# Sixteen batches of a stage written out instead of a two-batch loop, with every wait on a constant

## The reference, cut to what matters

```python
x = x + causal_attention(layernorm(x))     # stage 0: Q, K, V with bias, mask k <= q, softmax, Wo, bo
x = x + split_attention(layernorm(x))      # stage 1: a class per position, attention inside the class
x = x + rotary_attention(layernorm(x))     # stage 2: rotary q and k, softmax over all keys
x = x + split_attention(layernorm(x))      # stage 3: as stage 1
```

## Time and profile before

| | |
|---|---|
| median of 3 runs | 5199.68 us (5198.17 to 5214.73) |
| the profiled execution | 5192.83 us, of which its span is 5191.0 us |
| TensorE clock granted, mean | 0.953 |
| PE busy | 4514.9 us, 87% |
| DVE busy | 3178.9 us, 61% |
| ACT busy | 2550.6 us, 49% |
| POOL busy | 1655.2 us, 32% |
| DMA | 525.68 MB, of which 3.82 MB on queue 8 and 1.14 MB on queue 14 are of the kind "instruction" |

### The profile page before, as it was taken

One profiled execution on the slowest core, in us unless ns is written; L12 is line 12 of the kernel. 1 busy time (PEld: TensorE's weight loads), 2 busy tenths in 40 slices (PEclk: granted clock), 3 DMA queues, 4 the chain that ended last, 5 costly groups with the idle time before them and its releaser, 6 DMA issues. The chain is left out here.

```text
span 5191.0 us, 90278 instructions
## 1 busy us (share of the span) xinstructions
PE 4514.9 (87%) x26116; PEld 1909.3 (37%) x26116; DVE 3178.9 (61%) x6578; ACT 2550.6 (49%) x3362; POOL 1655.2 (32%) x922
## 2 busy tenths in 40 slices
PE   4988988899869999899995999999989599889889
PEld 2444444445413333333332333333333233333333
DVE  3545545455447667676663766666666277777776
ACT  1444444444435554455551655555555265555555
POOL 2354544545422434434434133332333300000000
PEclk8999999999979999999997999999999799999999
DMA  4343434344223334233232223323323322222221
GB/s 148 97 149 125 143 119 145 123 135 135 94 67 104 95 92 120 81 110 107 94 109 81 83 87 116 114 87 104 114 89 103 83 75 84 80 79 80 75 75 51
DMA packets 302300, 525.68 MB, mean 101 GB/s; under 512 B 58340, under 2 KB 236136, under 8 KB 285544
## 3 DMA queue, kind: packets, MB, share of 16 engines
q1 hardware_dynamic: 259432, 485.06, 31.5%
q10 hardware_dynamic: 42496, 35.66, 2.1%
HBM read 316.97 MB, written 201.46 MB: 100 GB/s over the span
## 5 line engine op out<-in xcount | busy, mean ns | idle before, releaser
L923 DVE TENSOR_REDUCE neg_max<-scores 128x1 f32<-128x512 f32 (+3 forms) x4096 | 2490.0, 636 | 1448.8 <-PE scores L1282 856.2
L1141 ACT ACTIVATE probs<-scores_t 128x1024 f32<-128x1024 f32 (+2 forms) x2048 | 1926.3, 947 | 1683.0 <-PE scores_t L1315 1193.9
L1282 PE MATMUL scores<-k_stack,q_stack 98*128 98x512 bf16 (+4 forms) x4096 | 1454.2, 378 | 311.0 <-DVE neg_max L923 216.5
L1315 PE MATMUL scores_t<-q_stack,k_stack 100*128 100x512 bf16 (+3 forms) x4096 | 1211.5, 370 | 130.6 <-DMA q_stack<-shift_rows 72.7
L1336 PE MATMUL o_ps<-probs,values 128*32 128x512 f32 (+1 forms) x8192 | 1039.7, 580 | 0.9 <-issue 0.6
L1282 PEld LDWEIGHTS scores<-k_stack,q_stack 96*128 96x128 bf16 (+1 forms) x4096 | 400.3, 98 | 1721.8 <-DVE neg_max L923 1243.9
L1315 PEld LDWEIGHTS scores_t<-q_stack,k_stack 100*128 100x128 bf16 x4096 | 382.3, 100 | 467.5 <-issue 292.1
L766 POOL TENSOR_TENSOR parts<-qk_f,parts 128x1024 bf16<-128x1024 f32 x128 | 272.3, 2128 | 707.8 <-ACT parts L1184 527.4
L779 POOL TENSOR_TENSOR x_res<-x_res,o_bias_s 128x1024 f32<-128x1024 f32 x32 | 75.6, 2364 | 1054.7 <-DMA x_res<-x_after 1054.7
L786 POOL TENSOR_TENSOR sim_inv<-sim_parts,minus_half 128x64 f32<-128x64 f32 x32 | 337.6, 10550 | 196.1 <-DVE sim_parts L1006 196.1
L737 POOL TENSOR_SCALAR var_eps<-mean_var 128x4 f32<-128x4 f32 x64 | 14.6, 229 | 1082.6 <-DVE mean_var L887 1082.6
(11 more groups left out here) (118 smaller groups left out, 4015.8 us busy)
## 6 DMA issues: line engine op xcount, KB each, us to landing
q_stack<-q_parts SPq DMA_DIRECT2D x1536, 64.0 KB, 2.5
values<-v_stage SPq DMA_DIRECT2D x64, 1024.0 KB, 4.2
values<-values SPq DMA_DIRECT2D x64, 1024.0 KB, 5.4
k_parts<-parts SPq DMA_DIRECT2D x192, 256.0 KB, 2.5
q_parts<-parts SPq DMA_DIRECT2D x192, 256.0 KB, 4.1
k_stack<-k_parts SPq DMA_DIRECT2D x256, 192.0 KB, 3.0
k_stack<-k_parts SPq DMA_DIRECT2D x256, 128.0 KB, 3.1
x_after<-x_res ACTq DMA_DIRECT2D x48, 512.0 KB, 2.9
```

The source lines that it names most:

```text
L923: nc.vector.tensor_reduce(neg_max[:, h % G, t:t + 1], bank[:, 0:n], AX.X, ALU.max, negate=True).then_inc(max_done.sem, 1)
L1141: nc.scalar.activation(probs[c][:, h % G, 0:n], st[i][:, 0:n], ACT.Exp).then_inc(exp_done.sem, 1)
L1282: last = nc.tensor.matmul(bank[:, 0:n], q[0:r, h, t * P:(t + 1) * P], k[0:r, h, 0:n], start=True, stop=kind != CAUSAL)
L1315: last = nc.tensor.matmul(st[i][:, off:off + L - q0], k[0:ROWS, h, kt * P:(kt + 1) * P], q[0:ROWS, h, q0:L], start=True, stop=kind != CAUSAL)
```

## The change

The loop of `run_stage` goes. All 16 batches of each stage are written out one after the other in the program of each engine. `Batch` loses its loop register, every wait is on a constant, every address is a constant, and the increments of "passed" are gone with their semaphore. The work, its order on each engine, the buffers and the tables are as they were. The two functions `loops` and `tail` go. The core of the diff:

```diff
     def __add__(self, k):
-        return Batch(self.s, self.n + k, self.turn)
-
-    def index(self):
-        return self.n if self.turn is None else self.turn * 2 + self.n
+        return Batch(self.s, self.n + k)
 
     def one(self):
-        return bass.ds(self.index(), 1)
+        return slice(self.n, self.n + 1)
...
-def wait_reg(eng, sem, value, still=None):
-    eng.wait_ge(sem, value)
-    if still is not None and not isinstance(value, int):
-        eng.sem_inc(still, 1)
...
     def after(self, B, *label):
-        lab = lambda n: (B.s, n) + label
-        if B.turn is None:
-            return self.at[lab(B.n)]
-        second = self.at[lab(B.n + 2)]
-        d = self.at[lab(B.n + 4)] - second
-        c = second - d
-        assert c > 0 and all(self.at.get(lab(B.n + 2 * i), c + d * i) == c + d * i for i in range(loops(B.s)))
-        return B.turn * d + c
-
-    def wait(self, eng, B, *label, still=None):
-        if B.turn is None and B.n < 0:
-            return
-        wait_reg(eng, self.sem, self.after(B, *label), still)
+        return self.at[(B.s, B.n) + label]
+
+    def wait(self, eng, B, *label):
+        if B.n >= 0:
+            eng.wait_ge(self.sem, self.after(B, *label))
...
             first(Batch(s, 0))
-            body(Batch(s, 0))
-            with eng.Fori(0, loops(s), 1) as i:
-                body(Batch(s, 1, i))
-                body(Batch(s, 2, i))
-            for n in tail(s):
+            for n in range(NB):
                 body(Batch(s, n))
             finish(Batch(s, NB - 1))
```

More of the change, by code:

```diff
@@ L188, with __init__ @@
 class Batch:
-    def __init__(self, s, n, turn=None):
-        self.s, self.n, self.turn = s, n, turn
+    def __init__(self, s, n):
+        self.s, self.n = s, n
     def __add__(self, k):
-        return Batch(self.s, self.n + k, self.turn)
-    def index(self):
-        return self.n if self.turn is None else self.turn * 2 + self.n
+        return Batch(self.s, self.n + k)
     def one(self):
-        return bass.ds(self.index(), 1)
+        return slice(self.n, self.n + 1)
     @property
     def begun(self):
[L206 to L214, removed]
-def wait_reg(eng, sem, value, still=None):
-    eng.wait_ge(sem, value)
-    if still is not None and not isinstance(value, int):
-        eng.sem_inc(still, 1)
+        return self.n > 0
 class Count:
@@ L233, in after, with wait_earlier, skip @@
     def after(self, B, *label):
-        lab = lambda n: (B.s, n) + label
-        if B.turn is None:
-            return self.at[lab(B.n)]
-        second = self.at[lab(B.n + 2)]
-        d = self.at[lab(B.n + 4)] - second
-        c = second - d
-        assert c > 0 and all(self.at.get(lab(B.n + 2 * i), c + d * i) == c + d * i for i in range(loops(B.s)))
-        return B.turn * d + c
-    def wait(self, eng, B, *label, still=None):
-        if B.turn is None and B.n < 0:
-            return
-        wait_reg(eng, self.sem, self.after(B, *label), still)
-    def wait_earlier(self, eng, B, back, *label, still=None):
-        v = self.after(B, *label) - self.step * back
[L253 to L260, removed]
+        return self.at[(B.s, B.n) + label]
+    def wait(self, eng, B, *label):
+        if B.n >= 0:
+            eng.wait_ge(self.sem, self.after(B, *label))
+    def wait_earlier(self, eng, B, back, *label):
+        v = self.after(B, *label) - self.step * back
+        if v > 0:
+            eng.wait_ge(self.sem, v)
+    def skip(self, eng, B, *label):
+        self.wait_earlier(eng, B, 1, *label)
         eng.sem_inc(self.sem, self.step)
@@ L536, in front_before @@
             if f == OWN:
-                if B.turn is None and B.n <= X_AHEAD:
+                if B.n <= X_AHEAD:
                     return (B + (-1), "xt") if B.n else (None, "")
                 return B + (-1 - X_AHEAD), "nx"
-            if B.s == 0 and (B.turn is not None or B.n + X_AHEAD < NB):
+            if B.s == 0 and B.n + X_AHEAD < NB:
                 return B + X_AHEAD, "xt"
@@ L573, in load_x @@
                 if B.begun:
-                    xn_done.wait(sp, B + (-1), OWN, still=still)
+                    xn_done.wait(sp, B + (-1), OWN)
                 sp.dma_start(x_new[:, :, :],
@@ L609, in load_next @@
                 if B.begun:
-                    st_full.wait(sp, B + (-1), H - 1, 1, still=still)
-                    qx_done.wait(sp, B + (-1), still=still)
+                    st_full.wait(sp, B + (-1), H - 1, 1)
+                    qx_done.wait(sp, B + (-1))
                 if B.s == 0:
-                    parts_out["k"].wait(sp, B + 1, OWN, still=still)
-                    parts_out["q"].wait(sp, B + 1, OWN, still=still)
+                    parts_out["k"].wait(sp, B + 1, OWN)
+                    parts_out["q"].wait(sp, B + 1, OWN)
                 load_stacks(B + 1)
@@ L618, in load_next @@
                 if B.begun:
-                    pv_done.wait(sp, B + (-1), NG - 1, T - 1, still=still)
+                    pv_done.wait(sp, B + (-1), NG - 1, T - 1)
                 if B.s == 0:
-                    v_out.wait(sp, B + 1, OWN, still=still)
+                    v_out.wait(sp, B + 1, OWN)
                 load_values(B + 1)
@@ L637, in store_parts @@
                 a, last = (0 if side == "q" else 2), prep_steps(kind_of(B, f))[-1]
-                prep.wait(sp, B, f, side, last, still=still)
+                prep.wait(sp, B, f, side, last)
                 to = parts_d[side][B.s + (f == NXT)][B.one()]
@@ L644, in store_values @@
             def store_values(B, f):
-                turn_free.wait(sp, B, FRONT[f][2], 1, still=still)
+                turn_free.wait(sp, B, FRONT[f][2], 1)
                 sp.dma_start(values_d[B.s + (f == NXT)][B.one()].rearrange("a p x -> (a p) x"),
@@ L654, in load_residual @@
             def load_residual(B):
-                stored.wait(sp, B + (-1), still=still)
+                stored.wait(sp, B + (-1))
                 if has_next(B.s):
-                    xn_done.wait(sp, B + (-1), NXT, still=still)
+                    xn_done.wait(sp, B + (-1), NXT)
                 sp.dma_start(x_res[:, :, :],
@@ L748, in prepare @@
                 both = lambda t: t[:, :].unsqueeze(1).broadcast_to([P, 2, L])
-                turn_free.wait(pool, B, FRONT[f][1], a + 1, still=still)
+                turn_free.wait(pool, B, FRONT[f][1], a + 1)
                 for step in steps:
-                    prep.wait_earlier(pool, B, 1, f, side, step, still=still)
+                    prep.wait_earlier(pool, B, 1, f, side, step)
                     if step == 0:
@@ L773, in bias_residual @@
             def bias_residual(B):
-                res_loaded.wait(pool, B, still=still)
+                res_loaded.wait(pool, B)
                 kind = STAGES[B.s]
@@ L884, in statistics @@
                 xn_done.wait_earlier(dve, B, 1, f)
-                wait_reg(dve, bn_done.sem, bn_done.after(B, f), still)
+                dve.wait_ge(bn_done.sem, bn_done.after(B, f))
                 for t in range(T):
@@ L905, in register_queries @@
                     dve.wait_ge(q_in[B.n % 2].sem, q_in[B.n % 2].after(B))
-                    if B.n >= 2 or B.turn is not None:
+                    if B.n >= 2:
                         sm_full.wait(dve, B + (-2), "extra")
@@ L958, in take_turn @@
                 kind = STAGES[B.s]
-                if B.turn is None and B.n < 0:
+                if B.n < 0:
                     turn_full.wait_earlier(dve, B, 0, k, i)
@@ L1059, in body @@
                         for k, off, i in turns_of(B.s, B.n, slot, place):
-                            if k in DVE_TURNS or B.n + off < 0 and B.turn is None:
+                            if k in DVE_TURNS or B.n + off < 0:
                                 take_turn(B + off, k, i)
```

23 lines of the change are left out of this document (11 added, 12 removed).

## The result

The changed kernel takes 5045.93 us (median; 5039.22 to 5059.16) where the kernel before, run beside it, takes 5198.93 us: a ratio of 0.9719 with a 95% interval of 0.9693 to 0.9745. The prediction was 5058 us. The profiled execution took 5051.34 us, with a span of 5049.7; the sum in the prediction gave 5052.

A forecast was written before the change was run, and what follows sets the result against it. PE, busy 87% of the span, bounds the kernel, with stalls at loop returns. 5192.83 less 127 us for returns and 14 for constants gives 5052, plus 6.85 to the median 5058 us; own range 5035 to 5080, 8-in-10 range 5008 to 5105.

The forecast's parts named there:

- The place: Where loops go back to their start, PE or DVE must fetch the loop's start again: 23 returns, together 127 us.
- rival 1: At loop returns, only the stalls themselves come back and what follows them stays: 90 us, 104 with constants, 5096 us; 12%.
- The size, stage by stage: Returns removed from the loops gain 62.8 us in stage 3, 37.2 in stage 2, 22.5 in stage 0, 4.7 in stage 1.
- the even batches that served as the plain measure: Batches starting inside the loop's body, behind no return, taken as a plain batch's cost: 82.42 us in stage 0.
- The constants: Waits on constants instead of registers, in the 54 batches in loops: 14 us gained, bounds 0 and 25 us.
- a return in stage 3 costs 10.5 us: Three times its stall, because shift rows then meet the 1024 KB load of values, and PE's granted clock falls.
- The copy at line 872: Sign in stage 1: DVE's copy, line 908 before the change, still takes over 2 us in most batches.
- queue 8 was to carry about 270 packets: Sign on the DMA queue taken for PE's program: about 270 packets, in stage 2 too.
- Blocks fetched late: Straight code outruns its fetches in stage 2, some 60 blocks at 3.3 us: 198 us, 5256 us in all; 4%.
- Stage 1 relieved: POOL's work ends sooner or shifts, catching fewer DVE copies: 89 us more, 4969 us (3%), or about half, 5014 us (15%).
- Something else that comes every second batch: The stalls at loop returns belong to something like a load, not the branch: 5185 to 5200 us; 4%.

The follow-up runs named there:

- the second profile: Kernel before and changed kernel, both unchanged, each profiled once more: 5194.72 us for the kernel before, 5059.25 us for the changed one.
- the loop of six: Kernel before with six batches in the loop's body in place of two, 4 returns in place of 23: 5086.28 us, ratio 0.98 to the kernel before.

## Why the prediction was right

*The place.* That returns of the loop are the loss is shown by the runs with one program written out: PE's in stage 3, DVE's in stage 2, and both in stage 0, where the prediction's rival 1 had counted PE alone. In stage 1 they show no gain for either. The chain of waits of the changed kernel has no piece of "issue" among its longest in stage 3, where it had the three of the earlier trace rows.

*The size, stage by stage.* The whole came out at 5051 us in the profiled execution where the sum gave 5052, and that is partly luck. Stages 2 and 3 came out within 2 us of the forecast, within 6 us in the second profile. Stage 0 gained 38 us where 26 were reckoned: the even batches that served as the plain measure weren't plain, 82.4 us where most straight batches take 81.1 to 81.4. How much of that was their waits on registers, and how much the returns, the runs part only roughly: batches 2 to 5 of stage 0 in the loop of six, on registers and with no return ahead, take 80.7 to 82.0 us. Stage 1 was reckoned at 8 us of gain and gave none. Slot 2 takes about 9 us in most of its batches now, where the even batches of the first profile of before had mostly 6.2 to 6.5 us. But the second profile of before has 9.2 to 9.4 us there in four of the seven even batches, batch 2 among them, so the measure was one execution's. Nor do the runs part returns from constants here: in the loop of six the five batches on registers with no return ahead have 9.2 to 9.3 us in slot 2, and with PE and DVE written out only about half of the batches do. The miss of 9 us is less than the 14.5 us between the two profiles of before. The two errors cancel.

*The constants.* 14 us were reckoned. 0.36 us in a batch of stage 2 would be 19 us for all 54 batches. That is within the bounds of 0 to 25, but rests on one batch.

*Why a return in stage 3 costs 10.5 us.* The sum was right, the reason given ahead of it only in part. The prediction put the excess over the stall on shift rows that meet the load of values, and on the clock. Slot by slot, against the even batches, the six returns of the first profile cost on average 3.1 us in slot 15, 4.0 us in slot 0, 0.5 us in slots 1 and 2, and 3.0 us in slots 3 and 4, where the shift rows are waited for; in the second profile it is 1.1 us there. So the larger part of the excess was slot 0: a second fetch and stall behind the first, which the prediction had in its rows (1.46 us of issue at 4321.33) and passed over here, and matmuls at half clock behind it.

*Signs that failed.* The copy at line 872 was to take over 2 us still in most batches of stage 1; it never takes over 0.29 us, though stage 1 is held as before. With the programs of PE and DVE written out alone, 13 of its 14 copies were still held, so it is writing out ACT, POOL and SP that moved this. And queue 8 was to carry about 270 packets; it carries 209. The 9 packets in two batches, from which that was reckoned, hold what a return fetches again, and the register arithmetic.

*The rivals.* Blocks fetched late: 39 blocks in the 14 batches of stage 2, where there had been 6, cost nothing, with batches there at 73.4 to 74.1 us. Stage 1 relieved: no. Only the stalls coming back: no, what followed them went as well. Something else that comes every second batch: no, writing out one engine's program took the loss away stage by stage.

## What to carry to other kernels

Look at the places where a loop goes back before you look for work to remove: idle "issue" time on one engine together with instruction packets on one queue was a fetch here, and PE and DVE each paid for their own. Whether a loop is held can depend on where its code lies, so some padding is worth a try where writing out is not wanted; 64 instructions cost 9 us once and saved some 50 us in stage 3. And when a stall is taken away, ask what it had been keeping apart: in stage 1 DVE waited more for POOL without the returns, and a small reordering on POOL was worth another 0.6% or so.

## What the runs showed of the hardware

- A return costs PE 2.4 to 3.5 us of issue in stage 3. The slot behind it takes 4.0 us more than plain in the loop of two batches, with a second stall in it, and 1.3 us more in the loop of six, without one. 64 instructions of padding took the fetches away altogether after the first turn; 256 changed nothing.
- 209 packets of 16 KB bring PE's 53638 instructions in straight code, 256 to a packet, and in batches 1 to 14 of stages 2 and 3 no "issue" longer than 0.8 us shows. A loop of 1671 instructions was held by PE, one of 1878 was not, and one of 1700 was or wasn't by its position.
- After such a stall PE's granted clock is at the lower of its levels, 1.2 GHz, for a few microseconds: 0.54 over slot 0 behind a return in the loop of two batches. In straight code it is 1.00 over all of stages 0, 2 and 3.
- DVE's cast and subtraction of 16 columns, 0.17 us when alone, end with the POOL instruction that runs beside them and take up to 2.26 us. With POOL's instructions halved, single waits fell to 1.1 us in slot 2, but both instructions waited again where one had been free.
